# Masks without a scale, x split as it is, and the first two batches in groups of one and two units

## The reference

```python
masks = (adj[None] == rel_ids[:, None, None, None])       # r b n m
h = einsum('rbnm,bmd->rbnd', masks, x)
y = einsum('rbnd,rdo->bno', h, weight) + bias
out = layernorm(x + y, axis=-1)                           # over D, eps 1e-5
```

## Time and profile before

| what | us |
|---|---|
| median of 3 runs (lowest, highest) | 124.0 (123.67, 124.12) |
| the profiled execution, its own time | 124.87 |
| its span from first to last instruction | 123.1 |
| PE, DVE, ACT, POOL busy in it | 106.7, 96.5, 87.4, 73.3 |
| read from memory, written | 37.81 MB, 4.19 MB |

### The profile page before, as it was taken

How to read it: one execution, slowest core, us unless ns; L and a number is a source line. 1 busy time by engine, 2 the same in 40 slices (tenths; PEclk the granted TensorE clock), 3 DMA queues, 4 the chain that set the end, 5 groups by cost and what they waited for, 6 DMA issues and landing times.

```text
span 123.1 us, 2783 instructions
## 1 busy us (share of the span) xinstructions
PE 106.7 (87%) x960; PEld 76.2 (62%) x974; DVE 96.5 (78%) x321; ACT 87.4 (71%) x106; POOL 73.3 (60%) x87
## 2 busy tenths in 40 slices
PE   6989992999599999999999999999999999999000
PEld 2369662768367676767676767676767677698000
DVE  1684736852998989899988998799969998798830
ACT  4098870999578949894989498949894989533310
POOL 2016000991293997399739983989398939809310
PEclk9999999999999999999999999999999999999755
DMA  4999999999999999999999999999999991040441
GB/s 124 361 362 414 414 405 410 407 390 430 407 416 387 420 418 397 415 418 421 404 408 418 418 415 375 432 426 418 384 428 426 421 359 46 0 170 0 170 156 33
DMA packets 12851, 42.23 MB, mean 343 GB/s; under 512 B 929, under 2 KB 7202, under 8 KB 9762
## 3 DMA queue, kind: packets, MB, share of 16 engines
q1 hardware_dynamic: 10432, 38.87, 79.5%
q10 hardware_dynamic: 2402, 3.15, 6.9%
HBM read 37.81 MB, written 4.19 MB: 341 GB/s over the span
## 4 chain that ended last, share of the span: by engine, by line
PE 64%; DMA 14%; SPq 9%; DVE 6%; issue 2%; ACT 0%; DVEq 0%
PE h_ps L591 36%; PE ids_t L577 17%; DMA x_sb<-x 14%; PE y_ps L605 10%; SPq L383 8%; DVE mask_t L690 2%; DVE row_max L666 1%; DVE rows L699 1%; DVE stats L705 1%; SPq L380 1%; PE ids_t L605 1%; DVE rows L744 0%; SPq L400 0%; DVE moments L711 0%; ACT std L506 0%
## 5 line engine op out<-in xcount | busy, mean ns | idle before, releaser
L489 ACT ACTIVATE junk<-adj_sb,minus 128x2048 bf16<-128x2048 int32 x32 | 63.8, 1995 | 1.4 <-issue 0.8
L690 DVE TENSOR_SCALAR mask_t<-ids_t,down 128x1024 bf16<-128x1024 uint16 x64 | 47.5, 743 | 7.8 <-PE ids_t L577 7.3
L577 PEld LDWEIGHTS ids_t<-ident,adj_sb 128*128 128x128 bf16 x512 | 36.9, 123 | 17.3 <-DMA adj_sb<-adj 4.7
L577 PE MATMUL ids_t<-ident,adj_sb 128*128 128x128 bf16 x512 | 40.3, 222 | 3.2 <-DMA adj_sb<-adj 3.1
L458 POOL TENSOR_SCALAR rows<-rows,rstd,shift 128x128 f32<-128x128 f32 x59 | 25.6, 451 | 17.8 <-DVE shift L737 17.8
L591 PE MATMUL h_ps<-mask_t,x_lo 128*128 128x512 bf16 (+2 forms) x160 | 33.4, 336 | 0.1
L591 PE MATMUL h_ps<-mask_t,x_hi 128*128 128x512 bf16 (+2 forms) x146 | 30.4, 332 | 2.4 <-DVE mask_t L690 1.3
L450 POOL TENSOR_TENSOR x_sb<-x_sb,bias_sb 128x1024 f32<-128x1024 f32 x8 | 19.0, 2377 | 7.4 <-DVE x_lo L750 7.3
L435 POOL TENSOR_TENSOR x_up<-x_sb,up 128x1024 f32<-128x1024 f32 x7 | 13.3, 1899 | 16.2 <-DVE up L684 16.1
L502 ACT ACTIVATE h_all<-h_ps 128x512 f32<-128x512 f32 (+2 forms) x20 | 10.2, 508 | 15.4 <-PE h_ps L591 15.4
L591 PEld LDWEIGHTS h_ps<-mask_t,x_hi 128*128 128x128 f16 x160 | 13.2, 98 | 9.2 <-DVE mask_t L690 2.2
(11 more groups left out here) (42 smaller groups left out, 33.3 us busy)
## 6 DMA issues: line engine op xcount, KB each, us to landing
adj_sb<-adj SPq DMA_DIRECT2D x24, 1024.0 KB, 20.4
adj_sb<-adj SPq DMA_DIRECT2D x16, 512.0 KB, 10.4
x_sb<-x SPq DMA_DIRECT2D x8, 512.0 KB, 18.7
out<-rows ACTq DMA_DIRECT2D x6, 512.0 KB, 7.4
out<-rows SPq DMA_DIRECT2D x1, 512.0 KB, 2.9
out<-rows SPq DMA_DIRECT2D x2, 256.0 KB, 3.7
w_sb<-weight SPq DMA_DIRECT2D x1, 64.0 KB, 5.7
bias_row<-bias ACTq DMA_DIRECT2D x1, 0.5 KB
```

The costliest lines, as they stand in the source:

```text
L489: nc.scalar.activation(junk[:, at % 2], adj_sb[:, slot, 2 * k:2 * k + 2, :], ACT.Square, scale=2.0, bias=minus[:, 0:1], accum_out=squares[ ...
L577: last = nc.tensor.transpose(bank[:, j, :], words[:, j // step(b), j % step(b), 0, :], ident[:, :])
L690: nc.vector.tensor_scalar(mask_t[:, b % 2, :, u * P:(u + 1) * P], ids_t[u % T_BANKS][:, :, :].bitcast(UINT16), down[:, b:b + 1], None, ALU ...
```

## The change

The scale is gone. `mask_unit` multiplies by the constant 1.0 and needs nothing but the transposes. `split_hi` on ACT is a plain cast of x to fp16 that waits for x itself, and `split_lo` is one subtraction (POOL; for batch 0 DVE, in two halves, as is its `split_hi`). `scale_maxima` is replaced by `row_maxima(b)`, which reads `x_hi` (fp16) and stands in the list of the first group of batch b itself (for batch 0 the fourth group, for the last batch between the masks of the second half). `find_far` now tests all row maxima against 1/8 and 2**15; outside of that the general pass runs. Batch 0 is in groups of 1, 1, 2, 2, 2 units and batch 1 in four groups of 2. Unit (0,0) is loaded ahead of x of batch 0, and six units of batch 1 come as three pairs. PE's warm-up matmuls are 6 and 2 instead of 9 and 1. ACT's checks follow a list of counts in the first 11 groups. In the tail `statistics` and `combine` stand one mask earlier.

```diff
-            return [(0, 1), (1, 1), (2, 2), (4, 4)] if b == 0 else ...
+        if b == 0:
+            return [(0, 1), (1, 1), (2, 2), (4, 2), (6, 2)]
+        if b == 1:
+            return [(0, 2), (2, 2), (4, 2), (6, 2)]
...
+        first = [1, 2, 2, 3, 4, 5, 6, 7, 8, 11, 13]
+        if g.index < len(first):
+            return first[g.index]
+        return min(PAIRS * (g.b + 1) + (2 if ends_batch(g) else 0), PAIRS * B)
...
+            load_unit(0, 0)
             load_x(0)
-            load_unit(0, 0)
             load_unit(0, 1)
...
             load_x(1)
-            for u in range(1, J):
-                load_unit(1, u)
+            load_unit(1, 1)
+            for k in range(1, PAIRS):
+                load_adj(1, k)
             load_x(2)
...
-            def scale_x(b):            # POOL
-                pool.wait_ge(s_scale, b + 1)
...
-                nc.gpsimd.tensor_tensor(x_lo[:, b % 2], x_up[:, :], x_hi[:, b % 2],
+                nc.gpsimd.tensor_tensor(x_lo[:, b % 2], x_sb[:, b % X_SLOTS], x_hi[:, b % 2],
...
-                act.wait_ge(s_scale, b + 1)
+                act.wait_ge(s_x[b % X_SLOTS], 16 * (b // X_SLOTS + 1))
...
-            idle_turns(9)
+            idle_turns(6)
...
+            def row_maxima(b):
+                dve.wait_ge(s_hi, b + 1)
+                nc.vector.tensor_reduce(row_max[:, b, :], x_hi[:, b % 2], AX.X, ALU.max,
                                         apply_absolute_value=True).then_inc(s_rm, 1)
...
-                                        down[:, b:b + 1], None, ALU.mult).then_inc(s_mask, 1)
+                                        1.0, None, ALU.mult).then_inc(s_mask, 1)
...
-                if early:
-                    scale_maxima(due)
+                if g.place == (3 if g.b == 0 else 0):
+                    row_maxima(g.b)
...
             mask_unit(a.b, GU)
             statistics(q)
+            row_maxima(a.b)
             mask_unit(a.b, GU + 1)
             sum_rows(last)
+            statistics(last)
             mask_unit(a.b, GU + 2)
-            statistics(last)
+            combine(r, last)
             mask_unit(a.b, GU + 3)
-            combine(r, last)
             find_far()
```

More of the change, by code:

```diff
@@ L100, in pair_no, with alone, pairs_checked_by @@
         return PAIRS * b + k
+    def alone(b, u):
+        return b == 0 or (b == 1 and u < 2)
     def loads_of(b, k):
-        return 16 * (b // ADJ_SLOTS + (1 if b % ADJ_SLOTS >= EARLY else 0))
+        return 16 * len([c for c in range(b % ADJ_SLOTS, b + 1, ADJ_SLOTS) if not alone(c, 2 * k)])
+    def pairs_checked_by(g):
+        first = [1, 2, 2, 3, 4, 5, 6, 7, 8, 11, 13]
+        if g.index < len(first):
+            return first[g.index]
+        return min(PAIRS * (g.b + 1) + (2 if ends_batch(g) else 0), PAIRS * B)
     ctx = ExitStack()
@@ L148, in adj_resnorm_kernel @@
         squares = sb("squares", [P, B * PAIRS], FP32)
-        far = sb("far", [P, B, J], FP32)
-        odd = sb("odd", [P, 2], FP32)
+        odd = sb("odd", [P, 3], FP32)
+        high = sb("high", [P, 1], FP32)
         worst = sb("worst", [P, 1], FP32)
@@ L173, in adj_resnorm_kernel @@
         s_biased = sem("bias_ready")
-        s_unit = [[sem(f"unit_loaded{b}{u}") for u in range(J)] for b in range(EARLY)]
+        s_unit = [[sem(f"unit_loaded{b}{u}") if alone(b, u) else None for u in range(J)] for b in range(EARLY)]
         s_x = [sem(f"x_loaded{n}") for n in range(X_SLOTS)]
@@ L491, in check, with split_hi @@
                                      accum_out=squares[:, at:at + 1]).then_inc(s_check, 1)
-            def split_hi(b):
-                act.wait_ge(s_scale, b + 1)
+            def split_hi(b, js, signal):
+                act.wait_ge(s_x[b % X_SLOTS], 16 * (b // X_SLOTS + 1))
                 if b >= 2:
                     act.wait_ge(s_prod, last_group_of(b - 2) + 1)
-                nc.scalar.activation(x_hi[:, b % 2], x_sb[:, b % X_SLOTS], ACT.Copy,
-                                     scale=up[:, b:b + 1]).then_inc(s_hi, 1)
+                    act.wait_ge(s_rm, b - 1)
+                nc.scalar.activation(x_hi[:, b % 2, js], x_sb[:, b % X_SLOTS, js], ACT.Copy).then_inc(signal, 1)
             def copy_h(g):
@@ L523, in _ @@
             act.preload_act_table(ACT.Sqrt)
-            act.wait_ge(s_const, 1)
-            split_hi(0)
+            split_hi(0, slice(0, HALF), s_hi0)
+            split_hi(0, slice(HALF, J), s_hi)
             act.wait_ge(s_spread, 1)
             nc.scalar.activation(bias_sb[:, :], y_ps[:, 0, :], ACT.Copy).then_inc(s_biased, 1)
+            act.wait_ge(s_const, 1)
             check(0, 0)
-            for g in groups[:LAST]:
+            for g in groups[1:LAST]:
                 b = g.b
[L531 to L541, removed]
+                copy_h(groups[g.index - 1])
+                if ends_batch(g):
+                    split_hi(b + 1, slice(0, J), s_hi)
                     if b >= 2:
                         store(sets[b - 2])
[L544 to L547, removed]
+                todo = range(pairs_checked_by(groups[g.index - 1]), pairs_checked_by(g))
+                for n, at in enumerate(todo):
+                    check(at // PAIRS, at % PAIRS)
+                    q = groups[g.index - 2] if g.index >= 2 else None
+                    if n == 0 and q and ends_batch(q):
+                        root(sets[q.b])
             a, c, e, d = groups[LAST:]
             copy_h(groups[LAST - 1])
-            check(a.b, 2)
-            check(a.b, 3)
+            for at in range(pairs_checked_by(groups[LAST - 1]), pairs_checked_by(a)):
+                check(a.b, at % PAIRS)
             copy_h(a)
@@ L746, in normalise, with split_lo @@
                 last.then_inc(s_done, 1)
[L748 to L751, removed]
+            def split_lo(b, js, hi, lo):
+                dve.wait_ge(hi, 1)
+                nc.vector.tensor_tensor(x_lo[:, b % 2, js], x_sb[:, b % X_SLOTS, js], x_hi[:, b % 2, js],
+                                        ALU.subtract).then_inc(lo, 1)
@@ L761, in find_far @@
-                dve.wait_ge(s_far2, 1)
-                nc.vector.tensor_reduce(odd[:, 1:2], far[:, :, :], AX.XY, ALU.max).then_inc(s_odd, 1)
+                dve.wait_ge(s_rm, B)
+                nc.vector.tensor_reduce(odd[:, 0:1], row_max[:, :, :], AX.XY, ALU.max).then_inc(s_odd, 1)
+                nc.vector.tensor_reduce(odd[:, 1:2], row_max[:, :, :], AX.XY, ALU.min).then_inc(s_odd, 1)
+                dve.wait_ge(s_odd, 2)
+                nc.vector.tensor_scalar(high[:, :], odd[:, 0:1], MOST, None, ALU.is_ge).then_inc(s_high, 1)
@@ L764, in find @@
+                dve.wait_ge(s_high, 1)
+                nc.vector.scalar_tensor_tensor(out=worst[:, :], in0=odd[:, 1:2], scalar=LEAST, in1=high[:, :],
+                                               op0=ALU.is_lt, op1=ALU.max).then_inc(s_worst, 1)
             def find():
                 dve.wait_ge(s_check, B * PAIRS)
[L767 to L770, removed]
+                nc.vector.tensor_reduce(odd[:, 2:3], squares[:, :], AX.X, ALU.max).then_inc(s_odd, 1)
@@ L778, in _ @@
             nc.vector.memset(minus[:, :], -1.0).then_inc(s_const, 1)
-            for part in (scale_maxima, scale_largest, scale_power, scale_down, scale_up):
-                part(0)
             mask_unit(0, 0)
-            split_lo(0)
+            split_lo(0, slice(0, HALF), s_hi0, s_lo0)
+            split_lo(0, slice(HALF, J), s_hi, s_lo)
             for g in groups[:LAST]:
@@ L818, in _ @@
                     shift_rows(r)
-                if due == 1:
-                    for part in (scale_maxima, scale_largest, scale_power, scale_down, scale_up):
-                        part(due)
             last, a, c, e, d = groups[LAST - 1:]
```

76 lines of the change are left out of this document (18 added, 58 removed).

## The result

| | before | changed |
|---|---|---|
| median, us (runs) | 124.01 (4) | 122.84 (4) |
| lowest to highest | 123.67 to 124.12 | 122.62 to 122.98 |
| profiled execution, us | 124.87 | 122.62 |
| its span, us | 123.1 | 120.8 |

The ratio is 0.9909, 95% interval 0.9885 to 0.9933: 1.17 us faster. The forecast was 123.3 (0.7 faster), range 122.4 to 124.5.

The account below looks back on a forecast made before the run. From 34 to 94 us PE and the load path were both full, then PE and DVE carried the tail. Of 2.5 us, 0.78 passes the loads; less 0.20 tail, plus 0.1 masks gives 0.7: 123.3, range 122.4 to 124.5.

Parts of the forecast that it names:

- the early 2.5 us: PE's gain near 33 us: 0.8 + 1.7 - 0.4, plus about 0.4 from a smaller project in arrears.
- steps 1 and 2: Early batches: masks free of x remove a 0.83 us wait; smaller groups in batches 0 and 1 save up to 1.7.
- the masks' step: Masks no longer wait for x: PE's mask waits of 0.83 us at 33 us and 0.24 at 95.9 go.
- steps 3 and 4: Middle loads: same bytes, counted nothing; pair (7,0) landing at 94.35 lets through 0.78 us, the other 1.7 becomes waits.
- step 6: Tail from 102: DVE's list to invert, now with batch 7's row maxima, needs 0.20 us more; 0.58 gained at invert.
- PE and DVE reach 113.1 together: Tail of the kernel before: PE's project ends at 113.07, DVE's sum that needs it starts at 113.12.
- the stream did not land later: Denies the slower rival: loads landing later at the head of batch 7, 124.8 with 1.5 us; 1 in 9.
- the cast of x was in time for the maxima: Denies part of the no-gain rival: row maxima wait for ACT's cast, masks queue behind, 124.0; 2 in 11.
- The lead at 102: Sign of the no-gain rival: PE's lead under 0.5 us there, the tail eats the gain, 124.0; 2 in 11.
- the first rival: Loads are no ceiling in the middle: PE keeps 2.5 us plus 0.2, less 0.2 in the tail, 121.5; 1 in 12.

Follow-up runs that it names:

- e5: Changed kernel with four adj units (last of batches 3 to 6, 0.5 MB each) not loaded; 121.34 us, ratio to before 0.9769.
- e11: Changed kernel with the earlier groups in batches 0 and 1 and four adj units of batches 3 to 6 not loaded; 123.38 us, ratio to before 0.9934.
- e0: The changed kernel run again, nothing altered; 122.89 us, ratio to before 0.9888.
- e6: The kernel before with four adj units (last of batches 3 to 6) not loaded; 123.97 us, ratio to before 0.9987.
- e7: Changed kernel with four slots of output rows instead of three and each store one batch later; 121.96 us, ratio to before 0.9814.
- e1: Changed kernel with the earlier groups in batches 0 and 1 and the earlier order of ACT's checks; 123.58 us, ratio to before 0.9926.
- e2: Changed kernel with DVE waiting for x of the next batch where the earlier row maxima stood; 123.08 us, ratio to before 0.9898.

## Why the prediction was right

123.3 was forecast and 122.84 measured: 1.17 us gained against 0.7.

*The masks and the groups, the early 2.5 us (steps 1 and 2).* Unit (2,0) was to be reached at 32.8 and was at 33.03, with 16 products of 256 columns owing. With the loads out of the way the lead is 2.37 us (e5). Of it 0.83 is there without the small groups (e11), against the 0.8 of the masks' step, and 1.54 is theirs, against 1.7. That the 0.83 is the masks' alone is not shown: no run takes back the other edits of the start. At the head of batch 3 (43.72) PE's weight side waited 1.0 us for its unit, so PE was level with the loads in time. The claim that the first products come a microsecond earlier was wrong (7.73 us, against 7.49 before), at no cost, since PE waits for loads behind it.

*The ceiling (steps 3 and 4).* (7,0) was to land at 94.35; it landed at 94.2, and PE waited for it. A lead of 0.78 us from there was forecast, 0.93 measured. The prediction takes off 0.1 for restarting from a wait; no row shows that cost and none is to be seen at 102. That the lead came out within 0.15 us is in part luck: in e0 it is 1.28, because (7,0) was there 0.35 us sooner. The waits for loads in the middle are 5.0 us on the weight side instead of some 1.5, but PE is busy for 58.71 of 60 and so loses 1.3. e5 and e6 bear the ceiling out.

*The tail (step 6).* +0.10 us was forecast (0.20 less 0.1 for the masks), -0.06 measured: from the first mask to `invert` 7.25 us against 7.31. The fp16 reduction took 1.20 us, as long as the fp32 one in the earlier trace rows (1.22 in the earlier trace rows), and the next mask starts 1.12 us after it, as taken; here the trace agrees with the Trainium skill, "VectorE: DVE Perf Modes", section "The perf-mode tier table", which gives the reduction one rate for all types. The masks gave their upper bound, 0.23 instead of 0.1. The final tests took 0.92 us instead of 1.10, 0.18 less where the forecast had 0.15. With the 0.77 us of DVE's idle time that went, 1.12 - 0.77 - 0.23 - 0.18 gives the -0.06. The sentence that PE and DVE reach 113.1 together was wrong: it took the `project` of group e for that of c, which was done at 111.90. It did not enter the sum.

*The sum.* The engines' end moved by 0.99 us against 0.68: 0.15 more of lead, 0.13 more from the masks in the tail and 0.03 from the tests. The prediction has nothing behind the engines, and there the last store is issued 0.3 us sooner after DVE's last pair than before. The 1.17 of the medians lies between 0.99 and 1.3; the landing of that store varies by more than what is left.

*The rivals.* Not one came about. The ceiling held; the stream did not land later; the cast of x was in time for the maxima. The lead at 102 was 0.93, not under 0.5. What the first rival would have given, e5 shows by leaving loads out: 2.6 us earlier at DVE's last pair than before, where the rival had 2.5.

## What to carry to other kernels

Before counting an early saving, measure at several later points how far each engine's use lags the landing of its load: the smallest lag is all that a saving can pass on (0.7 to 1.0 us of 2.4 here). Once the engine has caught up, look for bytes in that stream that could move later and for work on the tail's engine that could move earlier; here these gave about as much as the change itself, 1.1 to 1.3 us against 1.2. And in a tail of many like rows, tell them apart by their counts before building on who waits for whom.

## What the runs showed of the hardware

The longest landing of the last stores ranged from 3.2 (the changed kernel, e7) to 4.7 us (e11) in traces of nearly the same tail. A factor per partition in place of a constant costs DVE 57 ns on a mask of 128x1024 (744 against 687 ns). And PE's clock fell to 0.50, the lower of its two levels, in e1 after PE had waited 1.89 us for a load, but not in the kernel before after 2.35 us nor in e11 after 1.78; beside e11, e1's profiled execution lost 0.77 us while it was low. At 8 to 10 us it fell to 0.50 in e1, e2 and e5 and not in the other traces, which cost e2 and e5 nothing that can be seen at their end.
